# Joining the two halves of the token maxima on VectorE before TensorE turns them

## The reference

```
logits   = einsum('bnd,esd->bnes', xn, sn)              # token by slot
dispatch = softmax(logits, axis=1)                      # over the tokens
combine  = softmax(logits.reshape(b, n, e*s), axis=-1)  # over the 512 slots
slots    = einsum('bnd,bnes->besd', xn, dispatch)
h        = gelu(einsum('besd,edh->besh', slots, w1) + b1)
eo       = einsum('besh,ehd->besd', h, w2) + b2
out      = einsum('bmd,bnm->bnd', eo, combine)
```

## Time and profile before

| | |
|---|---|
| Median of 3 runs | 1065.32 us (1065.32 to 1065.45) |
| The profiled execution | 1065.09 us, of which the span from its first to its last instruction is 1063.3 us |
| TensorE matmuls (PE) | 1046.6 us busy, 98% of the span, 10266 instructions |
| TensorE weight loads (PEld) | 824.9 us, 78% |
| VectorE (DVE) | 918.8 us, 86% |
| ScalarE (ACT) | 810.7 us, 76% |
| GpSimd (POOL) | 414.3 us, 39% |
| Chain of work that ended last | PE 94%, DVE 2%, ACT 1%, issue 1% |
| Granted TensorE clock | 0.999 of 2.4 GHz over the span |
| `mx` on DVE | 48 times, 680 ns each |
| `mxT` on PE | 64 transposes, 286 ns each from start to modelled end |
| `rmax` on DVE | 16 times, 674 ns each |

### The profile page before, as it was taken

How to read it: one execution, slowest core, us unless ns; L and a number is a source line. 1 busy time by engine, 2 the same in 40 slices (tenths; PEclk the granted TensorE clock), 3 DMA queues, 4 the chain that set the end, 5 groups by cost and what they waited for, 6 DMA issues and landing times.

```text
span 1063.3 us, 27317 instructions
## 1 busy us (share of the span) xinstructions
PE 1046.6 (98%) x10266; PEld 824.9 (78%) x10266; DVE 918.8 (86%) x1818; ACT 810.7 (76%) x1434; POOL 414.3 (39%) x555
## 2 busy tenths in 40 slices
PE   7999999999999999999999999999999999999997
PEld 4578787877878778787787878778787787877866
DVE  4888988888998888898888988889988889988775
ACT  4577878778787787877778787886877878787775
POOL 2532434334353433534334443343534325343240
PEclk9999999999999999999999999999999999999999
DMA  6000000000000000000000000000000000000000
GB/s 263 12 11 2 2 22 2 21 2 11 12 2 21 2 15 8 2 21 2 21 2 2 22 2 21 2 11 13 2 21 2 21 2 1 23 1 11 2 12 10
DMA packets 18463, 16.85 MB, mean 16 GB/s; under 512 B 800, under 2 KB 17440, under 8 KB 18080
## 3 DMA queue, kind: packets, MB, share of 16 engines
q1 hardware_dynamic: 18336, 15.12, 4.4%
HBM read 10.93 MB, written 4.19 MB: 14 GB/s over the span
## 4 chain that ended last, share of the span: by engine, by line
PE 94%; DVE 2%; issue 1%; ACT 1%; POOL 0%; DVEq 0%; ACTq 0%; POOLq 0%
PE bank L1031 13%; PE bank L987 11%; PE bank L977 11%; PE bank_s L1008 7%; PE bank L997 6%; PE bank L968 5%; PE bank L938 5%; PE bank L833 3%; PE bank L931 3%; PE bank L864 3%; PE bank L960 3%; PE bank L918 3%; PE bank_s L1011 3%; PE bank L884 3%; PE bank L1038 3%; PE bank L1046 2%
## 5 line engine op out<-in xcount | busy, mean ns | idle before, releaser
L326 POOL TENSOR_TENSOR ret_abs<-ret_abs 128x512 f32<-128x512 f32 x128 | 182.3, 1427 | 250.8 <-ACT ret_abs L479 250.6
L659 DVE TENSOR_TENSOR ret<-bank_s,k_sb 128x1536 f32<-128x1536 f32 x128 | 223.7, 1748 | 29.8 <-PE bank_s L1011 20.2
L479 ACT ACTIVATE ret_abs<-ret 128x1536 f32<-128x1536 f32 x128 | 189.6, 1481 | 26.5 <-DVE ret L659 26.5
L987 PEld LDWEIGHTS bank<-w_sb,hact 128*128 128x128 f32 x1024 | 127.9, 191 | 18.0 <-issue 7.8
L987 PE MATMUL bank<-w_sb,hact 128*128 128x128 f32 x1024 | 138.6, 278 | 0.0
L333 POOL TENSOR_SCALAR dT<-dT,drec 128x256 f32<-128x256 f32 x128 | 67.0, 541 | 170.2 <-DVE drec L723 170.2
L977 PE MATMUL bank<-slotsT,w_sb 128*128 128x128 f32 x1024 | 130.1, 275 | 0.4 <-ACT slotsT L469 0.4
L977 PEld LDWEIGHTS bank<-slotsT,w_sb 128*128 128x128 f32 x1024 | 123.2, 192 | 1.7 <-ACT slotsT L469 0.8
L474 ACT ACTIVATE hact<-hact 128x512 f32<-128x512 f32 x128 | 80.2, 628 | 52.1 <-DVE hact L728 51.7
L1031 PE MATMUL bank<-ret,vrow 128*32 128x256 f32 (+1 forms) x2048 | 108.2, 329 | 0.3 <-POOL ret_abs L326 0.3
L1031 PEld LDWEIGHTS bank<-ret,vrow 128*32 128x32 f32 x2048 | 59.9, 109 | 42.0 <-issue 2.5
(11 more groups left out here) (145 smaller groups left out, 2274.2 us busy)
## 6 DMA issues: line engine op xcount, KB each, us to landing
x_sb<-x SPq DMA_DIRECT2D x16, 256.0 KB, 2.7
w_sb<-w SPq DMA_DIRECT2D x2, 2048.0 KB, 14.0
out<-attn SPq DMA_DIRECT2D x16, 256.0 KB, 2.3
v_sb<-vectors SPq DMA_DIRECT2D x1, 705.0 KB, 7.3
k_sb<-consts SPq DMA_DIRECT2D x1, 538.0 KB, 6.1
w_sb<-weights SPq DMA_DIRECT2D x1, 512.0 KB, 4.4
w_sb<-weights SPq DMA_DIRECT2D x1, 320.0 KB, 3.2
slot_sb<-slot_rows SPq DMA_DIRECT2D x1, 256.0 KB, 3.3
```

The source lines that it names most:

```text
L326: pool.tensor_tensor(both[:, :, P:SEQ], both[:, :, P:SEQ], both[:, :, SEQ:3 * P], ALU.add)\
L479: act.activation(ret_abs[:, q % MR], ret[:, q % MR], ACT.Abs).then_inc(ready["ab"].sem, 1)
L659: dve.tensor_tensor(ret[:, q % MR], bank_s[:, :, 0:3 * P], causal.unsqueeze(1).broadcast_to([P, Q, 3 * P]), ALU.mult)\
L987: ins = pe.matmul(bank[:, i * C:(i + 1) * C], hact[:, i, c], w2_sb[:, e, c], start=(c == 0), stop=(c == HC - 1))
```

## The change

After `mx` 2, VectorE takes one more maximum, of the lower 64 partitions of `mx` with the upper 64, in place on the lower 64. A semaphore of its own, `mxh`, tells that it is done. TensorE then transposes 64 partitions instead of 128, into 64 columns for each tile of tokens instead of 128, and `rmax` reduces 256 columns instead of 512. `mxT` and `cs` wait for `mxh` where they waited for `mx` 2. `ORDER` and `BANK` are unchanged, and no step is moved.

```diff
                 dve.tensor_tensor(mx[:], mx[:] if i else cT[:, 0], cT[:, i + 1], ALU.max).then_inc(ready["mx"].sem, 1)
+                if i == 2:
+
+                    dve.wait_ge(*ready["mx"](p, 2))
+                    dve.tensor_tensor(mx[0:P // 2], mx[0:P // 2], mx[P // 2:P], ALU.max).then_inc(ready["mxh"].sem, 1)
...
-                dve.tensor_reduce(rmax[:], bank[:].rearrange("p (j s) -> p j s", j=TILES), X, ALU.max, negate=True)\
+                dve.tensor_reduce(rmax[:], bank[:, 0:TILES * P // 2].rearrange("p (j s) -> p j s", j=TILES), X, ALU.max, negate=True)\
...
             def cs(p, par, m):
...
-                dve.wait_ge(*ready["mx"](p, 2))
+                dve.wait_ge(*ready["mxh"](p))
...
             def mxT(p, par, k):
-                pe.wait_ge(*ready["mx"](p, 2))
+                pe.wait_ge(*ready["mxh"](p))
                 bank = claim("mxT", p)
                 for j in range(TILES):
-                    ins = pe.transpose(bank[:, j * P:(j + 1) * P], mx[:, j * P:(j + 1) * P], ident)
+                    ins = pe.transpose(bank[:, j * P // 2:(j + 1) * P // 2], mx[0:P // 2, j * P:(j + 1) * P],
+                                       ident[0:P // 2, 0:P // 2])
```

More of the change, by code:

```diff
@@ L213, in build @@
             ("ab", QUADS), ("add", QUADS), ("usq", DUOS), ("den", DUOS), ("dsq", DUOS), ("ug", DUOS),
-            ("rx", DUOS), ("ln", 1), ("rs", 1), ("gated", 2), ("attn", 2), ("LTc", 4), ("mx", 3), ("rmax", 1), ("rBc", 1), ("cs", 4), ("ce", 4),
+            ("rx", DUOS), ("ln", 1), ("rs", 1), ("gated", 2), ("attn", 2), ("LTc", 4), ("mx", 3), ("mxh", 1), ("rmax", 1), ("rBc", 1), ("cs", 4), ("ce", 4),
             ("ltmax", 4), ("DTe", 4), ("drec", 4), ("dn", 4), ("Dc", 4), ("slc", 2), ("hb", E), ("hg", E),
```

## The result

The changed kernel takes 1076.06 us (median of 5 runs, 1075.98 to 1077.37), the kernel before 1065.35 us beside it. The ratio is 1.0101, 95% interval 1.0089 to 1.0113: it is 10.7 us slower, where 9.2 us were forecast. The range of the prediction, 1069.5 to 1078.0, holds it; it is 1.6 us above the 1074.5, so outside the 1 us around it to which the forecast gave 0.56. The profiled execution has a span of 1074.1 us, that is 10.8 more than before.

The account below looks back on a forecast made before the run. TensorE was taken to bound the kernel. Fourteen middle pairs at 0.42 + 0.14 = 0.56 us (7.8), 0.75 in pair 0 and 0.72 in pair 15 made 9.3 us, hence 1074.5 us, range 1069.5 to 1078.0.

Parts of the forecast that it names:

- 0.42 us late: At `mxT` in a middle pair: waiting for the join, it starts at 500.49 in place of 500.07.
- The slack: Between the end of `mx` and the start of `mxT` in a middle pair: 0.2 to 0.3 us to spare.
- I take 0, as `global` has the full width that the new transposes keep: Inside `mxT`: weight loads set the pace, so four narrower transposes save 0, within bounds of 0 and 0.22 us.
- Rival 2: In `mxT`, the stream sets the pace and loads shrink: 1072.9 with the change of tiling (0.06), 1069.3 without (0.05).
- If the loads came closer together: Sign of being wrong: the weight loads of the four transposes in `mxT` should still come 0.11 us apart.
- The tiling: From `mxT` into `e`: leaving a tile of 64 rows costs 0.13 to 0.14 us a pair, bounds 0 and 0.21.
- All these cost nothing: Steps behind the join: 0.72 us of delay to `ret` 2, and up to that to `rBc`, is covered at `quad` 3 and `score` 0.
- The first pair and the last: Pair 0 loses 0.75 us at `mxT` with the change of tiling; pair 15 loses 0.72 at `quad` 3, behind `ret` 2.
- The dearer join (3): On VectorE, the join takes 0.1 to 0.5 us more than `mx`; at 0.25 that gives 1078.5; chance 0.12.
- the cheap one (4): On VectorE, the join takes 0.34 us for half the partitions, a pair loses 0.22: 1069; chance 0.03.
- Nothing was gained (5): Rival: VectorE reaches `mx` 2 earlier by 0.42 us or more, narrower transposes give up to 0.22 a pair: 1061.8; chance 0.03.
- A tile without a price (1): Behind `mxT`, no change of tiling, or one that costs nothing: 7.2 us slower, 1072.5; chance 0.15.

Follow-up runs that it names:

- the bursts: Seven bursts of ten transposes or matmuls each, added behind the last step of the kernel before; 0.107 us between transposes, 0.213 us per float32 matmul load.

## Why the prediction was right, and where not

**The join and its place.** "0.42 us late" and 0.68 for the join were right: 0.416 and 0.69. The slack was read rightly too: the change of tiling and not `mx` held `mxT` back before.

**The saving: "I take 0, as `global` has the full width that the new transposes keep".** This step failed. `global` is an ordinary float32 matmul, whose load takes twice a transpose's, as the bursts show. So the 0.115 us of the earlier trace rows didn't carry over. In the changed kernel the transposes come 0.11, 0.06 and 0.06 apart, where they came 0.16, 0.11 and 0.11 apart before, which saves 0.147 us. The row was of the wrong kind of load. Rival 2, with the change of tiling, had a saving here, of 0.11 us; but it took the load to shrink with its rows, and that the bursts exclude. "If the loads came closer together" was one of the prediction's own signs of being wrong, and it came true. What the prediction makes of the Trainium skill went too far in two places. The earlier trace rows has loads of 128 rows alone, and so can't agree that rows don't count. And the 0.22 us is half of the 0.44 us of the earlier trace rows; by the formula that the Trainium skill ("TensorE: Matmul & The Clock Gate", Back-to-back issue gap) gives for the full clock, N/2.4 + 2.5 ns for N columns, my estimate is 0.027 us less for each transpose and 0.11 for the four. Measured was 0.147.

**The tiling.** +0.14 was forecast and 0.145 measured, and the narrow transposes without the join confirm it. With the saving of 0.147, narrow transposes give nothing.

**"All these cost nothing."** This step failed as well, at one of the covers that I should have looked at. I followed the delay of `ret` 2 to `quad` 3, to `rBc` and `score` 0, and these were covered as I said. I didn't ask who waits for `eTc`, which stands in ScalarE's list between `ab` 2 and `rBc`. `rB` does, by its claim of bank 2, whose last reader is `eTc`. Before, `eTc` ended at 503.50 and `rB` started at 503.73; at a latency of 0.14 that left some 0.08 us, against a delay of 0.72. It cost +0.245, and the same chain another 0.022 at `o` 1 through `Dc` 1.

**The two together.** The missing saving and the missing wait, -0.15 and +0.27, offset each other by more than half: 0.56 us forecast and 0.68 measured a pair. That the forecast came this close is partly luck. With the wait alone in its sum it would have said 14 x 0.27 = 3.8 us more, 1078.3, and with the saving alone 16 x 0.147 = 2.4 us less, 1072.1. The forecast's account of the loss (mostly the wait of `mxT`) is also not the whole one: with that wait taken away, the loss stays at 10.5 us; with the wait at `rB` taken away it falls by about 3 us, to 8.1; only with both gone, and the small one at `o` 1, does it vanish.

**The first pair and the last.** Pair 0 loses 0.61 at `mxT` and 0.12 at `rB`, 0.72 in all (forecast 0.75). In pair 15 `quad` 3 starts 0.71 later from the last transpose on, less the 0.147 saved: 0.56 (forecast 0.72).

**Rivals.** The dearer join (3) and the cheap one (4) are out by its 0.69 us. Nothing was gained (5): `mx` 2 came no earlier. A tile without a price (1) is out by the run of the narrow transposes alone.

## What to carry to other kernels

An instruction that is put in front of others on an in-order engine has two kinds of waiters: who waits for it, and who waits for anything behind it, however many engines further on. Walk the second list step by step, with every claim of a shared buffer in it, before you write that a delay is covered; here the cover was 0.08 us thick. Where two waits hang on one delay, one behind the other, the loss was here the larger of the two (0.64 us at `rB`) and not the sum of what each costs alone (0.42 more), so taking away the first one showed next to nothing.

On TensorE, take the price of a weight load from a row of the same kind, and count the change of tiling on both sides before you make an operation narrower.

## What the runs showed of the hardware

A transpose's weight load of 128 columns takes half of that of an ordinary float32 matmul at a granted clock of 0.50: 0.107 us (with 64 and with 32 rows) and 0.213 us (with 128 and with 64 rows). At full clock the transposes of 64 partitions come 0.062 us apart and those of 128 partitions 0.109. Since fewer rows changed nothing in any burst, I take it that the streamed columns set the pace of the second; a transpose of 128 rows that streams fewer columns was not run.

Behind the last transpose on a tile of 64 rows the next matmul starts 0.044 us later than behind one of 128, although only half the columns stream, and the one after it another 0.101 later. That is as much as an ordinary matmul pays behind `quad`, on tiles of 32 rows (0.10, against the earlier trace rows).

A join of partitions 0 to 63 with 64 to 127 takes 0.69 us for 512 columns, and `mx`, the same operation on 128 partitions without the crossing, 0.68: reading two halves of the partitions costs 0.01 us at most, unless 64 partitions without it are faster than 128, of which no run has the row.

Where a TensorE step waits for the last reader of its bank, its first weight load came 0.115 us after that reader's end, with the reader on ScalarE (`rB` for `eTc`, `o` 1 for `Dc` 1) and on VectorE (`DT` 1 for `rmax`, `global` for `attn` 1) alike.
